# A four-layer diffusion transformer on one core: statistics in two pieces, top-k masking on VectorE, a new order of work

## The reference

```
scores = einsum('bqhd,bkhd->bhqk', q, k) / sqrt(16)
top_s, top_i = top_k(scores, 16)
attn = softmax(top_s, axis=-1)
o = einsum('bhqk,bhqkd->bqhd', attn, v gathered at top_i)
```

## Time and profile before

| | before |
|---|---|
| median of 3 runs | 2931.4 us (2920.38 to 2933.68) |
| the profiled execution | 2928.1 us |
| its span, first to last instruction | 2925.9 us |
| PE busy / DVE / ACT / POOL | 94% / 64% / 48% / 24% |
| mean granted clock of TensorE | 0.976 |

### The profile page before, as it was taken

The page is one execution under the profiler, slowest core; times in us unless marked ns, Lnnn a source line. Parts: engine busy times, 40 slices in busy tenths (PEclk is TensorE's granted clock), DMA queues, the critical chain, the costliest instruction groups (busy, mean ns, idle before and its releaser), DMA issues.

```text
span 2925.9 us, 47617 instructions
## 1 busy us (share of the span) xinstructions
PE 2736.6 (94%) x15077; PEld 1352.8 (46%) x15133; DVE 1884.0 (64%) x4177; ACT 1415.4 (48%) x2575; POOL 711.6 (24%) x1063
## 2 busy tenths in 40 slices
PE   8999999999989998999988898899899998999899
PEld 5344344335535324334455566666554423224456
DVE  6977387643565874866354688668966784885620
ACT  4454635574455683566644343323123584775431
POOL 2100001131331111231134455443411010112420
PEclk9999999999999999999999999999999999999899
DMA  6233023323542312332166526421501322113621
GB/s 212 59 110 116 29 71 100 102 77 92 169 147 53 116 49 72 94 109 70 50 194 181 147 83 191 126 83 61 164 23 33 101 63 56 45 53 111 182 89 38
DMA packets 268152, 286.78 MB, mean 98 GB/s; under 512 B 70665, under 2 KB 207243, under 8 KB 267275
## 3 DMA queue, kind: packets, MB, share of 16 engines
q1 hardware_dynamic: 256651, 282.28, 32.8%
q0 software_dynamic: 11264, 1.46, 0.3%
HBM read 167.43 MB, written 114.72 MB: 96 GB/s over the span
## 4 chain that ended last, share of the span: by engine, by line
PE 69%; DVE 12%; issue 7%; DMA 6%; POOL 3%; SPq 2%; ACT 1%; DVEq 0%; ACTq 0%; POOLq 0%
PE ring_c L1457 12%; PE ring_b L1424 12%; PE ring_a L1380 10%; PE ring_b L1480 7%; PE ring_a L1492 7%; PE ring_b L1423 3%; PE ring_a L1469 3%; PE ring_b L1337 3%; DVE row_max L1743 2%; PE ring_a L1480 2%; DMA q_ring<-neg_max_parts 2%; PE ring_b L1451 1%; PE ring_b L1412 1%; DVE topk_marks L1768 1%; DVE topk_marks L1762 1%
## 5 line engine op out<-in xcount | busy, mean ns | idle before, releaser
L1565 ACT ACTIVATE probs<-ring_b 128x512 f32<-128x512 f32 (+1 forms) x1728 | 918.0, 600 | 414.1 <-PE ring_b L1424 352.2
L1743 DVE TENSOR_REDUCE row_max<-ring_a 128x1 f32<-128x1024 f32 x512 | 601.8, 1216 | 156.3 <-PE ring_a L1380 154.8
L1424 PE MATMUL ring_b<-q_ring,k_ring 100*128 100x512 bf16 x1536 | 525.5, 380 | 15.6 <-ACT probs L1565 2.8
L1380 PE MATMUL ring_a<-k_ring,q_ring 96*128 96x512 bf16 x1536 | 448.3, 382 | 30.5 <-DVE row_max L1743 15.9
L1457 PE MATMUL ring_c<-probs,v_and_ones 128*17 128x512 f32 x3072 | 403.0, 600 | 1.5 <-ACT probs L1565 0.9
L1856 POOL CAST neg_max_parts<-neg_max 16x128 bf16<-16x128 f32 x112 | 34.8, 310 | 1329.6 <-ACT neg_max L1559 1133.5
L1740 DVE CUSTOM_DVE_ANT_0 w_mlp<-ring_a,w_mlp 128x1024 bf16<-128x1024 f32 x256 | 302.0, 1221 | 62.6 <-PE ring_a L1380 61.8
L1424 PEld LDWEIGHTS ring_b<-q_ring,k_ring 100*128 100x128 bf16 x1536 | 145.0, 97 | 346.3 <-issue 236.1
L1380 PEld LDWEIGHTS ring_a<-k_ring,q_ring 96*128 96x128 bf16 x1536 | 134.7, 98 | 256.5 <-issue 159.8
L1480 PE MATMUL ring_b<-h_feat,w_mlp 128*128 128x512 f32 x512 | 233.1, 601 | 9.5 <-issue 9.0
L1787 DVE TENSOR_TENSOR x_tok<-x_tok,ring_a 128x512 f32<-128x512 f32 x96 | 65.5, 684 | 255.9 <-PE ring_a L1492 161.8
(11 more groups left out here) (144 smaller groups left out, 3503.9 us busy)
## 6 DMA issues: line engine op xcount, KB each, us to landing
q_ring<-scr_q SPq DMA_DIRECT2D x128, 384.0 KB, 4.3
scr_q<-split SPq DMA_DIRECT2D x64, 384.0 KB, 2.9
k_ring<-scr_k SPq DMA_DIRECT2D x64, 384.0 KB, 5.4
scr_q<-split SPq DMA_DIRECT2D x64, 256.0 KB, 3.1
scr_out<-out_stage SPq DMA_DIRECT2D x128, 128.0 KB, 2.4
scr_out<-out_stage SPq DMA_DIRECT2D x64, 256.0 KB, 3.0
h_feat<-scr_out SPq DMA_DIRECT2D x56, 256.0 KB
reciprocals<-scr_recip SPq DMA_DIRECT2D x56, 256.0 KB
```

Of the source, the lines that this page charges most:

```text
L1380: last = mm(ps[:, half * BLOCK:(half + 1) * BLOCK], q[0:PARTS, h, t * P:(t + 1) * P], k_view(g)[0:PARTS, h, half * BLOCK:(half + 1) * BLOC ...
L1424: last = mm(ps[:, :], k_view(g)[0:ROWS, h, s.kt * P:(s.kt + 1) * P], q[0:ROWS, h, q0:q0 + BLOCK], start=not g.masked, stop=True)
L1565: f(PT[0:n, s.pt, :], ps[0:n, :], ACT.Exp, **kw).then_inc(b_evac, 1)
L1743: v.tensor_reduce(NM[:, s.nm, s.u:s.u + 1], ps, AX.X, ALU.max).then_inc(a_evac, 1)
```

## The change

Statistics are computed in two `stats` steps of two tiles each; the first waits for the x step u = 0 only. `tk_mark` is cut into `tk_half` (first eight) and `tk_mark` (next eight). POOL's part, now `tk_shift`, follows `tk_half` and is the subtraction alone. `tk_exp` follows it. A new DVE step `tk_mask` waits for the exponentials and the marks, and multiplies the exponentials by (S3 <= 0.9 GONE), which is 1 for a chosen key and 0 for another. `tk_turn` waits for it, and S3 is free only after it. All ranks have new values, and POOL's reach goes from 0.1 to 0.3.

```diff
 RANK (all 16 kinds), SECOND, LATER: new values; of layer 2 for instance
-    prep=(5, -9, 0, 10.4),          load=(18.2, -1.2, 4.8, 0.8),
-    tk=(-0.5, -1.5, -4.5, 5.5),     win_f=(-1.3, -9.3, -6.3, 1.7),
+    prep=(-2, -5, -9, 21),          load=(20, 4.3, 24, -0.8),
+    tk=(-12, -10, -10, -10),        win_f=(6, -12, 6, 6),
-REACH = dict(PE=0.0, ACT=0.2, DVE=0.1, POOL=0.1, SP=0.2)
+REACH = dict(PE=0.0, ACT=0.2, DVE=0.1, POOL=0.3, SP=0.2)
...
-            src = fl.x[blk][-1]
-            s = yield do("stats", [("DVE", 1.85)], after=[src], counts=["stat_n"], l=l, i=i, b=b, blk=blk, src=src)
+            for u in range(2):
+                src = fl.x[blk][u]
+                s = yield do("stats", [("DVE", 0.95)], after=[src], counts=["stat_n"], l=l, i=i, b=b, blk=blk, src=src, u=u)
...
-                s = yield do("tk_mark", [("DVE", 5.95)], after=[k, s3_last], counts=["tk_n"], of=k, s3=s3, s3_last=s3_last)
-                p.spawn(topk_rest(st, key, g, unit, k, s), rank_of("tk_s", st.l, st.b, st.blks[0]))
+                half = yield do("tk_half", [("DVE", 2.95)], after=[k, s3_last], counts=["half_n"], of=k, s3=s3, s3_last=s3_last)
+                p.spawn(topk_rest(st, key, g, unit, k, half), rank_of("tk_s", st.l, st.b, st.blks[0]))
+                s = yield do("tk_mark", [("DVE", 2.95)], after=[half], counts=["tk_n"], of=k, half=half)
+                p.raise_flag(key + ("marked", g.n, hp), s)
...
-        s = yield do("tk_args", [("POOL", 5.23)], after=[mark], counts=["tkarg_n"], of=k, mark=mark)
-        p.give("S3", mark.s3, s)
+        s = yield do("tk_shift", [("POOL", 1.37)], after=[half], counts=["tkarg_n"], of=k, half=half)
         e = yield do("tk_exp", [("ACT", 0.605)], after=[s], counts=["tkexp_n"], of=k, arg=s, fn="exp")
+        mark = yield ("flag", key + ("marked", g.n, k.hp))
+        e = yield do("tk_mask", [("DVE", 0.75)], after=[e, mark], counts=["tkmask_n"], of=k, e=e, mark=mark)
+        p.give("S3", half.s3, e)
...
+                elif s.kind == "tk_mask":
+                    k = s.of
+                    dve.wait_ge(tk_sel, s.mark.tk_n + 1)
+                    dve.wait_ge(tk_exp, s.e.tkexp_n + 1)
+                    v.scalar_tensor_tensor(out=TS[:, k.ts], in0=S3[:], scalar=GONE * 0.9, in1=TS[:, k.ts], op0=ALU.is_le, op1=ALU.mult)\
+                        .then_inc(tk_masked, 1)
...
-                elif s.kind == "tk_args":
+                elif s.kind == "tk_shift":
                     k = s.of
-                    pool.wait_ge(tk_sel, s.mark.tk_n + 1)
-                    link(g_.tensor_scalar(S3[:], S3[:], GONE * 0.9, -1.0e30, ALU.is_gt, ALU.mult))
+                    pool.wait_ge(tk_half, s.half.half_n + 1)
                     m = M8[:, k.ts, :, 0:1].broadcast_to([P, 8, CTX])
-                    link(g_.tensor_tensor(out=TS[:, k.ts], in0=TS[:, k.ts], in1=m, op=ALU.subtract))
-                    g_.tensor_tensor(out=TS[:, k.ts], in0=TS[:, k.ts], in1=S3[:], op=ALU.add).then_inc(tk_arg, 1)
+                    g_.tensor_tensor(out=TS[:, k.ts], in0=TS[:, k.ts], in1=m, op=ALU.subtract).then_inc(tk_arg, 1)
                     pool.wait_ge(tk_arg, s.tkarg_n + 1)
```

More of the change, by code:

```diff
@@ L283 @@
 RANK = dict(
[L284 to L299, removed]
+    init=(17.3, -1.5, -5.5, 15.3),
+    mod=(-4.4, -8, -0.4, -6),
+    prep=(-2, -5, -9, 21),
+    out=(-2, -12, 6.8, -12),
+    ctx=(17.0, 19, 17.0, 15.7),
+    load=(20, 4.3, 24, -0.8),
+    cross_f=(11.3, 13.3, 4.1, 4.1),
+    cross_s=(3.3, -2.1, 1.8, -6.2),
+    mlp=(-5.8, 12.0, 4.0, -0.4),
+    self_f=(-12, 14.8, -1.1, 7.8),
+    self_pv=(4.1, 22, 0.1, 23),
+    self_s=(-9, 14.2, -12, 7.2),
+    tk=(-12, -10, -10, -10),
+    tk_s=(-5.2, -6.2, -6.2, -6.2),
+    win_f=(6, -12, 6, 6),
+    win_s=(5.1, 3.1, 5.7, 5.1),
 )
-REACH = dict(PE=0.0, ACT=0.2, DVE=0.1, POOL=0.1, SP=0.2)
+REACH = dict(PE=0.0, ACT=0.2, DVE=0.1, POOL=0.3, SP=0.2)
 DELAY = (7.5, 40)
[L303 to L306, removed]
+SECOND = dict(init=-1, mod=14, prep=-4, out=12, ctx=-19, load=-7, cross_f=10,
+              cross_s=15, mlp=-11, self_f=5, self_pv=24, self_s=-7, tk=-11, tk_s=-12,
+              win_f=-19, win_s=-12)
+LATER = (3, -3.5, -38, -36)
 FILL_ONE = 0.11
@@ L320, in plan @@
         p.pool(name, n)
-    flow = [Step(x=[[None], [None]], before=[None, None], wo_users={}, w2_users={}, cq_users={}, w1_users={}) for _ in range(BATCH)]
+    flow = [Step(x=[[None, None], [None, None]], before=[None, None], wo_users={}, w2_users={}, cq_users={}, w1_users={}) for _ in range(BATCH)]
     def init():
@@ L752, in topk_units, with topk_rest @@
                 s3, s3_last, _ = yield ("get", "S3")
-                s = yield do("tk_mark", [("DVE", 5.95)], after=[k, s3_last], counts=["tk_n"], of=k, s3=s3, s3_last=s3_last)
-                p.spawn(topk_rest(st, key, g, unit, k, s), rank_of("tk_s", st.l, st.b, st.blks[0]))
+                half = yield do("tk_half", [("DVE", 2.95)], after=[k, s3_last], counts=["half_n"], of=k, s3=s3, s3_last=s3_last)
+                p.spawn(topk_rest(st, key, g, unit, k, half), rank_of("tk_s", st.l, st.b, st.blks[0]))
+                s = yield do("tk_mark", [("DVE", 2.95)], after=[half], counts=["tk_n"], of=k, half=half)
+                p.raise_flag(key + ("marked", g.n, hp), s)
             p.give("Q", g.q, k)
-    def topk_rest(st, key, g, unit, k, mark):
-        s = yield do("tk_args", [("POOL", 5.23)], after=[mark], counts=["tkarg_n"], of=k, mark=mark)
-        p.give("S3", mark.s3, s)
+    def topk_rest(st, key, g, unit, k, half):
+        s = yield do("tk_shift", [("POOL", 1.37)], after=[half], counts=["tkarg_n"], of=k, half=half)
         e = yield do("tk_exp", [("ACT", 0.605)], after=[s], counts=["tkexp_n"], of=k, arg=s, fn="exp")
+        mark = yield ("flag", key + ("marked", g.n, k.hp))
+        e = yield do("tk_mask", [("DVE", 0.75)], after=[e, mark], counts=["tkmask_n"], of=k, e=e, mark=mark)
+        p.give("S3", half.s3, e)
         places = yield ("many", "PT", 2, 2 if unit.scores else 4)
@@ L1008, in blocks_kernel @@
         pool_g = sem("gated_weights_and_biases")
-        tk_sel, tk_arg, tk_exp = sem("top_k_marked"), sem("top_k_arguments"), sem("top_k_exps")
+        tk_half, tk_sel = sem("top_k_first_half"), sem("top_k_marked")
+        tk_arg, tk_exp, tk_masked = sem("top_k_arguments"), sem("top_k_exps"), sem("top_k_masked")
         stats_ready, root_ready = sem("statistics_ready"), sem("inverse_roots_ready")
@@ L1427, in _ @@
                 elif s.kind == "tk_turn":
-                    pe.wait_ge(tk_exp, s.e.tkexp_n + 1)
+                    pe.wait_ge(tk_masked, s.e.tkmask_n + 1)
                     ps = need_b(s.bn)
@@ L1637, in _ @@
                     st, mv = STAT[:, s.b, s.blk], MV[:, s.b, s.blk]
-                    for t in range(4):
+                    for t in range(s.u * 2, s.u * 2 + 2):
                         last = v.bn_stats(st[:, t, :], X[:, s.b * TILES + s.blk * 4 + t, :])
                     link(last)
-                    for t in range(4):
+                    for t in range(s.u * 2, s.u * 2 + 2):
                         last = v.bn_aggr(mv[:, t, :], st[:, t, :])
@@ L1752, in _ @@
                     v.tensor_copy(TS[:, s.ts], ps[:, :, 0:CTX]).then_inc(a_evac, 1)
-                elif s.kind == "tk_mark":
+                elif s.kind == "tk_half":
                     k = s.of
@@ L1759, in _ @@
                     if s.s3_last is not None:
-                        dve.wait_ge(tk_arg, s.s3_last.tkarg_n + 1)
+                        dve.wait_ge(tk_masked, s.s3_last.tkmask_n + 1)
                     for i in range(8):
                         last = v.match_replace(S3[:, i, :], M8[:, k.ts, i, :], TS[:, k.ts, i, :], GONE)
-                    link(last)
+                    last.then_inc(tk_half, 1)
+                elif s.kind == "tk_mark":
+                    dve.wait_ge(tk_half, s.half.half_n + 1)
                     for i in range(8):
```

1 line of the change is left out of this document (removed).

## The result

The changed kernel takes 2937.3 us in the median of 20 runs (2932.8 to 2948.5), the kernel before 2926.3 us (2919.6 to 2939.4). The ratio is 1.0034, 95% interval 1.0023 to 1.0045: about 10 us or 0.3% slower, inside the range, but on the other side of zero from the forecast 2899. The profiled execution took 2935.0 us with a span of 2932.7, against 2928.1 and 2925.9.

What follows compares the result with a forecast made beforehand. PE's slack, 430 us idle and filled, was all any order could win, most densely in the top-k stretch bound through POOL and DVE. Terms -11 - 11 + 14 - 5 - 19 = -32: 2896 against 2928.1, median 2899, range 2845 to 2948.

Steps and rivals of the forecast that it cites:

- (a): Top-k loop: POOL leaves it, so marks reach the next unit's match sooner; -11 us, ends -18 and 0.
- (b): Top-k stretch: DVE operations no longer held up beside POOL's removed ones; -11 us, ends -20 and 0.
- (c): Mask on DVE, 0.80 us each, 17 units counted on the chain; +14 us, ends +5 and +51.
- (d): Norms: half the statistics run during the second x step; -6 for seven norms, +1 for links, ends -11 and +5.
- (e): New order: a fifth of the 96 us gained if top-k slack fell to 11%; -19 us, ends -96 and +35.
- DVE waiting for ACT: Rival in top-k: the mask and DVE work behind it wait for ACT's exponential; 2984 at worst, 2956 likely, chance 0.18.
- Hidden: Rival: PE's other chains take over, leaving only contention, mask and statistics; 2926 us, range 2917 to 2946, chance 0.18.
- the spacing: Sign of being right: top-k units that follow each other 7 to 8 us apart instead of 10.2.
- the two DVE operations: Sign of being right: L1692 and L1693 in the top-k stretch average under 0.75 and 0.55 us.
- slack in the stretch: Sign of being right: PE's idle plus fills in the top-k stretch at 120 to 140 us instead of 156.
- DVE's wait before the mask: Sign of being wrong: DVE idle before the mask with ACT as releaser, over 20 us in total.
- the same top-k stretch with more slack in the self-attention stages: Sign of being wrong: it would say that the order and not the top-k chain decided.

Runs made afterwards that it cites:

- the added operation of the experiment: Kernel before, order kept, plus one DVE scalar_tensor_tensor of 616 columns per top-k unit that leaves the marks unchanged: 1.0052, 15 us slower.
- the three parts in the order of before: Kernel before, order kept, with POOL's shorter part, the mask's work and early statistics together, without the mask's waits: 0.9967, 10 us faster.
- near orders of the same steps: Ranks moved at random by at most 2 or 1 in the changed kernel, 2914.9 and 2937.3 us; by at most 1 in the kernel before, 2916.2 and 2928.7.
- searched: Changed kernel's steps with ranks found by a longer random search over the planner alone, against the kernel before: 2884.7 us, 0.9859.
- the near order that beats before: Changed kernel with every rank moved by a random amount of at most 2, against the kernel before: 2914.9 us, 0.9954.
- exchanged: Changed steps under the ranks of before, 2946.4 us (1.0062); steps of before under the changed kernel's ranks, 2989.8 us (1.0209).

## Why the prediction was wrong

(a) and (b), POOL out of the loop and the contention, together -22: right in sign and some 7 us too small. In the same order they gave -29, interval -35 to -23. But of the 26 us by which the span fell, 20 are PE's busy time, with a higher clock, and the sum had no such term (last section). So it is partly luck that the size comes so near.

(c), the mask, +14: +15 for an operation of this size at another place. One mask takes 0.83 us in the changed kernel where 0.80 was taken, so the earlier trace rows were the right rows; the added operation of the experiment took 0.95, and half of its 30.3 us reached the end, which fits 17 of 32 units on the chain. The sentence on the shared read interface was borne out once in the changed kernel, in its timeline:

```profile
1956.81 2.36 POOL L1861 TENSOR_TENSOR x_tok<-x_tok,gate 128x1024 f32<-128x1024 f32 x1
...
1957.81 2.02 DVE L1782 SCALAR_TENSOR_TENSOR topk_scores<-topk_marks,topk_scores 128x616 f32<-128x616 f32 x1
```

POOL's addition ended at 1959.17 and the mask at 1959.83, so it stood still until the other was over. The Trainium skill ("SBUF — State Buffer", Who interferes with whom) says just that of a VectorE instruction with two SBUF inputs; the run agrees. A standstill of this length happened to one mask of 32, so it decided nothing.

(d), statistics, -5 (-6 for the norms, +1 for the links): not borne out; the early piece in the order of before gave 2 us slower, interval 2 faster to 6 slower. The count of norms on the chain was of those whose bn_stats ended last; what the early piece itself delays on DVE was left out.

(e), the order, -19: this is the step that failed. I wrote that the planner "now knows of a loop shorter by 5 us a unit" and took a fifth of the slack for it. But the planner's own end came only 2.4 us earlier with all of the change in it. Under the old ranks the new steps even end 12.2 us later in the plan (2830.1 for 2817.9), and a better set of ranks for the same steps gives 29.6 us (2815.5 to 2785.9). What the chip adds to a plan was 9.2 us more for this order than for before's. In place of -19 the runs leave +20, the result less the -10 of the three parts in the order of before; that holds the mask's waits as well as the order. The sign is a property of one draw among many orders: near orders of the same steps are up to 22 us apart, more than (a) to (d) together, and one of them is faster than before. My ends for (e), -96 and +35, held the value, but the -19 was a hope drawn from the slack, and the chance of 0.64 for faster had the same fault: it treated the sum's sign as that of its largest guess. With a term of zero and a spread of 10 us, parts (a) to (d) would have given 2928 - 13 = 2915 for the profiled execution, and "within 0.5%" a little likelier than "faster by over 0.5%".

The rivals: DVE waiting for ACT happened (20.0 us). It doesn't decide between orders, for about the same wait goes with the fastest kernel (18.1 us, searched) and with the near order that beats before (19.0); what it costs all of them was not measured. "Hidden", 2926, is nearest in size, but for another reason: in the old order POOL's shorter part was worth 29 us, so other chains did not hide it there. The signs named in the prediction came out so: POOL's fall, POOL gone from the chain between top-k steps, the spacing, the two DVE operations (0.69 and 0.53 us, under 0.75 and 0.55) and the mask's length right; slack in the stretch at 164, not 120 to 140. Of the signs of being wrong, DVE's wait before the mask stood at its limit. The other, "the same top-k stretch with more slack in the self-attention stages", came true in part: slack outside the stretch rose by 12 us, but the stretch itself got shorter by 40, and in which stages the 12 us lie was not read.

## What to carry to other kernels

When a change comes with a new order, price the edit in the old order and the order by itself: keep the instruction lists fixed for the one, and shuffle near-ties for the other. A planner's gain below the scatter between its plans and the chip (here some 8 us on 2900) says nothing about one kernel, while gaps of 20 us or more between plans were found again on the chip, so the effort belongs in a longer search. Ranks fit only the steps that they were found for: exchanged, they cost 8 and 61 us. And an experiment that prices an edit in the old order must keep the edit's waits, not only its work, or it leaves them mixed with the order.

## What the runs showed of the hardware

With the same instruction lists, the kernel with POOL's shorter part alone finished its matmuls in less busy time on PE. The page of that kernel, and its top-k stretch, beside the earlier trace rows:

```profile
PE 2716.6 (94%) x15077; PEld 1342.4 (46%) x15133; DVE 1866.7 (64%) x4177; ACT 1414.7 (49%) x2575; POOL 588.0 (20%) x999
```
```profile
1640.00:2180.00 540.00, 495.27 (x3052) 329.41 (x3053) 413.67 (x1926) 182.10 (x295) 125.23 (x136) 0.99 0.37 110
```

15077 matmuls took 2716.6 us instead of 2736.6, with the same fills, and the granted clock of the stretch was 0.99 where it had been 0.96 (of its two levels, 2.4 and 1.2 GHz, the lower one held for about 2% instead of 8% of the stretch). PE had stood still there for 44.7 us instead of 53.9. So of 26 us of span that this edit gave, 20 are PE's own busy time and 6 its idle time. Over the whole execution the mean granted clock was 0.982 where it had been 0.976. I had not counted that.

That the removed waits raised the clock is argued from these rows and not shown. With all three edits in the same order PE's busy time was 2735.4 us at a mean clock of 0.975, as in the kernel before, though PE's wait for the exponential was gone there too (0.9 us).
